# Attention phases of three tiles: the maxima pass before, or after, the score passes on TensorE

## The reference

```python
h = layernorm(layernorm(x)) * ln_scale + ln_bias
c_q, c_kv = h @ w_down_q.T, h @ w_down_kv.T            # 256 -> 128
q, k, v = (c @ w.T split in 16 heads of 64)            # q, k then turned by rope tables
scores = einsum('bhqd,bhkd->bhqk', q, k) / 8           # 1024 x 1024 for each head
attn = softmax(scores, axis=-1)
out = (attn @ v joined) @ w_out.T + residual
```

## Time and profile before

| | us |
|---|---|
| median of 3 runs (4092.33 to 4099.59) | 4095.67 |
| the profiled execution | 4098.04 |
| its span, first to last instruction | 4096.1 |
| attention, about 522 to 3590 of the span | 3068 |

### The profile page before, as it was taken

How to read it: one execution, slowest core, us unless ns; L and a number is a source line. 1 busy time by engine, 2 the same in 40 slices (tenths; PEclk the granted TensorE clock), 3 DMA queues, 4 the chain that set the end, 5 groups by cost and what they waited for, 6 DMA issues and landing times. The chain is left out here.

```text
span 4096.1 us, 65749 instructions
## 1 busy us (share of the span) xinstructions
PE 3897.4 (95%) x24908; PEld 2207.7 (54%) x24908; DVE 2849.5 (70%) x3796; ACT 2536.2 (62%) x3191; POOL 2932.8 (72%) x1632
## 2 busy tenths in 40 slices
PE   7999979999999999999999999999999999989999
PEld 6888834444444444444444444444444444478888
DVE  5656567777777776777778777767776777565563
ACT  4455446766766676667666766766676666645544
POOL 3444448878877897888788878878887888634443
PEclk9999989999999999999999999999999999999999
DMA  3233221111211221121122212211211121142331
GB/s 123 99 124 109 81 93 53 60 55 59 83 53 53 71 66 53 61 81 53 53 66 76 63 53 66 68 50 60 86 55 53 58 79 62 33 145 76 125 114 63
DMA packets 192772, 300.36 MB, mean 73 GB/s; under 512 B 50328, under 2 KB 100937, under 8 KB 191817
## 3 DMA queue, kind: packets, MB, share of 16 engines
q1 hardware_dynamic: 192456, 296.17, 22.3%
HBM read 201.20 MB, written 26.73 MB: 56 GB/s over the span
## 5 line engine op out<-in xcount | busy, mean ns | idle before, releaser
L1088 DVE TENSOR_REDUCE atNM<-atPS 128x2 f32<-128x1024 f32 x1024 | 1225.7, 1219 | 452.8 <-PE atPS L899 450.1
L1029 ACT ACTIVATE atPT<-atPS 128x1024 f32<-128x1024 f32 x1024 | 1014.0, 1024 | 773.1 <-PE atPS L920 766.7
L1187 POOL TENSOR_TENSOR atACC<-atACC,atPT 128x1024 f32<-128x1024 f32 x510 | 1238.7, 2429 | 89.3 <-ACT atPT L1029 39.1
L931 PE MATMUL atPO<-atPT,atV 128*64 128x512 f32 x4096 | 1014.2, 602 | 0.0
L1187 POOL TENSOR_TENSOR atACC<-atPT 128x1024 f32<-128x1024 f32 x255 | 606.6, 2379 | 262.8 <-PE atOT L953 181.7
L1020 ACT ACTIVATE atPS<-atSH 128x1024 f32<-128x1024 f32 x683 | 687.4, 1023 | 50.8 <-DVE atNM L1088 34.0
L920 PE MATMUL atPS<-atQH,atKL 64*128 64x512 f32 x2048 | 459.9, 445 | 66.3 <-DVE atPS L1094 51.7
L931 PEld LDWEIGHTS atPO<-atPT,atV 128*64 128x64 f32 x4096 | 259.0, 136 | 456.5 <-issue 433.1
L899 PE MATMUL atPS<-atKH,atQH 64*128 64x512 f32 x2048 | 444.0, 431 | 10.0 <-ACT atQH L1009 7.9
L1094 DVE COPY atPS<-atSH 128x1024 f32<-128x1024 f32 x341 | 418.7, 1228 | 37.9 <-DMA atSH<-atMD 11.4
L920 PE MATMUL atPS<-atQH,atKH 64*128 64x512 f32 x2048 | 406.6, 393 | 0.0
(11 more groups left out here) (278 smaller groups left out, 6461.5 us busy)
## 6 DMA issues: line engine op xcount, KB each, us to landing
atSH<-atMD SPq DMA_DIRECT2D x128, 512.0 KB, 4.3
atVT<-atR SPq DMA_DIRECT2D x508, 128.0 KB, 2.1
f1GB<-f1GD SPq DMA_DIRECT2D x128, 256.0 KB, 6.7
f2GB<-f2GD SPq DMA_DIRECT2D x128, 256.0 KB, 6.8
atRSUM<-atRD SPq DMA_DIRECT2D x126, 256.0 KB, 4.0
X<-x SPq DMA_DIRECT2D x4, 1024.0 KB, 6.0
XS<-x SPq DMA_DIRECT2D x16, 256.0 KB, 3.6
x<-X SPq DMA_DIRECT2D x16, 256.0 KB, 2.3
```

The costliest lines, as they stand in the source:

```text
L931: ins = pe.eng.matmul(PO[HI[h], :], V[n % 2][:, j, HI[h]], PT[k % NPT][:, h, :], start=j == 0, stop=j == T - 1)
L1029: act.eng.activation(PT[k % NPT][:, :, :], PS[ring.of[step]][:, :, :], ACT.Exp, scale=SCALE).then_inc(grown.sem)
L1088: dve.eng.tensor_reduce(NM[:, q // 4, :, q % 4, t], PS[ring.of[step]][:, :, :], AX.X, ALU.max, negate=True).then_inc(most_out.sem)
L1187: pool.eng.tensor_tensor(total[:, :, :], begun[:, :, :], PT[k % NPT][:, :, :], ALU.add).then_inc(gathered.sem)
```

## The change

Within each phase PE's order becomes

- first half: M0, S0, S1, the others of `x`, one attend;
- second half: S2, M1, M2, the others of `x+1`, two attends, the others of `x+2`.

```diff
             for x in range(-42, 2 * PER * (NN + 4), 3):
-                order += tile("score", x) + most_of(x) + tile("fill", x + 2) + tile("score", x + 1)
+                order += most_of(x) + tile("fill", x + 2) + tile("score", x) + tile("score", x + 1)
                 order += others_of(x) + held + tile("attend", x - 1)
                 order += gathers(held + tile("attend", x - 1))
-                order += most_of(x + 1) + tile("score", x + 2) + most_of(x + 2)
+                order += tile("score", x + 2) + most_of(x + 1) + most_of(x + 2)
                 now, held = tile("attend", x), tile("attend", x + 1)
```

## The result

The changed kernel takes 4202.05 us (median of 4 runs, 4194.91 to 4205.81) against 4097.14 for the kernel before on the same chip: 1.0255 times the time, 95% interval 1.0238 to 1.0273. That is 105 us slower. The direction was forecast, the size was not: 4132 was predicted, with 4172 as the upper end.

What follows compares the result with a forecast made beforehand. PE bounds it, at 95% busy, so time changes through PE's waits. Terms in 48 tiles: -1.7 + 0.9 + 1.7 + 1.1 - 0.3 = +1.7 us, times 21.3 is +36 us: 4132; range 4106 to 4170 (0.50).

Steps and rivals of the forecast that it cites:

- (a): Wait of S2 for DVE's fill shrinks in phases 0, 3, 15, 30, 33: 1.7 us less in 48 tiles.
- (c): Others' one bank is read later behind M1's reduction, phases 9, 18, 27, 33, 42: 1.7 us more in 48 tiles.
- (b): S2's wait where a raise ends the phase before, phases 9, 21, 27, 36, 39: 0.9 us more in 48 tiles.
- (d): S1 waits for its fill behind both later reductions, phases 39, 18, 33: 1.1 us more in 48 tiles.
- Much slower: Rival: late readings push each other, (b) and (c) feeding each other; doubled (c) and (d) give 4192; chance 0.12 (over 4170).
- Faster: Rival: (a) decides, (c) and (d) vanish: 4073 us, or 4053 without (b) as well; chance 0.28.

Runs made afterwards that it cites:

- The second half alone: Kernel before with only the second half of a phase reordered (S2, M1, M2), forerunners kept: 4217.9 us, ratio 1.0285.
- the combined kernel: First half of the change, second half as before, low part on POOL, copy for phase 18 one tile ahead, against before: 4030.0 us, ratio 0.9835.
- second copy experiment: After, with the copy of the queries' high part for M0 of phase 18 one tile earlier: 4188.6 us, ratio 1.0221.
- the first copy try: After, with the copy of the queries' high part for the pair that begins in phase 0 one tile earlier: 4199.6 us, ratio 1.0257.
- the halves taken apart: Each half's new order alone, against before: first half 4098.9 us, ratio 1.0003; second half 4217.9 us, ratio 1.0285.
- after with the short subtraction: After, with the low part of the queries (L1083) over 64 columns, not 1024, from the third pair of heads on: 4154.6 us.

## Why the prediction was right or wrong

**Right in direction and in its largest loss.** The mechanism was that M1 behind S2 makes all that follows on DVE later. The second half alone shows it with 120 us, the rows of phases 9 and 42 to 0.1 us.

**(a), the gain, is the step that failed first.** I took 1.7 us less in 48 tiles. By the table, phases 0, 3, 15, 30 and 33 changed by +0.27, +0.04, +0.33, -0.23 and +0.29. Of these, 33 also held 0.15 and 0.25 of losses forecast; what is left is 0.3 longer, so there was no gain. The wait of S2 did shrink where I said, and the combined kernel has 1.4 of the 1.7. The whole change is 3.6 us in 48 tiles over the forecast. Phases 21, 36 and 3, where the low part of the queries stretches, hold 2.0 of that, and phases 15 and 0, where a maxima step waits for the copy of the queries, 1.2. What ate the gain:

- In phase 15 M0 met the copy of the queries, 0.55 us each time (second copy experiment, 13 us). I followed what comes later through M1, and not what M0, moved forward, has to wait for besides its bank pair.
- In phase 3 I let the low part of the queries, and all behind it up to the sum, move forward with the fill. It started 0.52 us earlier and ended 0.24 later, since it waits for POOL's addition, which ends later. Freed of that, the phase would still have lost: with the low part on POOL the sum waits 0.7 us, because its raise is read behind the same late reductions as in phase 9. I applied (c) in phases 9, 27 and 33 and not there.
- In phase 0 the kind that should have gained 0.53 lost 0.54. Its M2 is the first maxima of its pair, and it stands 1.1 us behind M1 instead of 0.23, waiting for the copy:

```profile
2482.30 1.05 ACT L1009 ACTIVATE atQH<-atU 128x1024 fp32r<-128x1024 f32 x1
...
2483.50 0.50 PE L899 MATMUL atPS<-atKH,atQH 64*128 64x512 f32 x2 [0.72 <-ACT atQH L1009]
```

  With this copy one tile earlier (the first copy try) M2 still starts 0.9 us behind M1, now for the exponential that the copy pushed back, and the phase shrinks by only 0.09 us. ACT is the limit there, in either of these orders.

**(b) was mis-sized by the low part of the queries.** For phases 9, 27 and 39 it came as worked out to about 0.1 us (in 39, the 0.23 of M1 whole, where I had taken 0.10). For 21 and 36 I took 0.32 and 0.15 and it was 0.76 and 1.03. I priced L1083 at one recorded duration, 1.93 us, and moved it as if that were its own. Its length depends on where POOL stands, and in the slow phases the new order puts its start 0.06 to 0.6 us behind the start of an addition. With the low part on POOL, 21 and 36 lose nothing: all of (b) there is the collision. Net of phase 3 it is 21 us in the whole kernel.

**(c) and (d) were right**: phase 9 +1.06 for 0.97, phase 42 +0.90 for 0.8, 27 +0.37 for 0.28; only 18 lost less, 0.26 for 0.65, since S1's fill was in time there.

**The rivals.** "Much slower" gave 4192, near to the result, in part for another reason: (b) and (c) did not feed each other, since phases 12 and 24, right behind delayed ones, are unchanged to 0.02 us. It was the missed waits. But that rival did name the low part of the queries, and the forecast did not follow it up. "Faster" is out by the result; the halves taken apart show that (a) gained nothing even by itself. My remark that 0.1 us a phase makes 34 us named the true size of the risk; the range did not follow it.

## What to carry to other kernels

When a step is moved forward, list all that it waits for, not only the wait that it is meant to shorten. Apply a mechanism, once found, to every place of the period. An instruction whose durations in a trace spread from 1.2 to 3.0 us has no price of its own; find what it waits for before moving it: here that was more than half of what the forecast missed.

## What the runs showed of the hardware

A DVE subtraction with both inputs and its output in SBUF does not run beside a POOL addition that is under way: it waits for that instruction's end. In the trace of after, 44 of the 64 runs of L1083 start while POOL is at work, and each of them ends 1.08 or 1.09 us after POOL's instruction did; the other 20 take 1.21 or 1.22. Over 64 columns (after with the short subtraction) it ends 0.08 or 0.09 us after POOL's. The wait is inside the recorded duration (1.21 to 3.41 us, and 0.21 to 2.41 for 64 columns) and is not shown as idle time.

It goes both ways. In the trace of before, 32 of POOL's 765 additions take 3.15 to 3.32 us and not 2.38. All of them start while L1083 runs, and end 2.2 to 2.3 us after its end. An example, in which L1083 started between two additions:

```profile
1942.53 5.83 POOL L1187 TENSOR_TENSOR atACC<-atACC,atPT 128x1024 f32<-128x1024 f32 x2
...
1944.89 1.22 DVE L1083 TENSOR_TENSOR atQL<-atU,atQH 128x1024 fp32r<-128x1024 f32 x1
```

DVE's reductions and copies on PSUM beside the same additions keep to 1.22 and 1.23 us (at most 1.23 in some 1000 of them). The Trainium skill has this ("SBUF — State Buffer", SBUF: two separate sides): a DVE instruction with two SBUF inputs and a GpSimd instruction that reads SBUF share a port pair as an exclusive lock, whoever starts first holds it for the whole instruction. The trace agrees. Had I read L1083's spread beside it, the collision would have been a term of the sum.
